# A graph layer on one core: output weights' halves added beside the ranking, and one block for storing the sums and the output

## The reference

```python
agg = segment_sum(res, col, num_segments=n) + segment_sum(res_i, row, num_segments=n)
h = jnp.concatenate([agg, agg], axis=1)
o = typed_linear(h, Wa, ba, node_type)      # Wa: (19, 512, 256), ba: (19, 256)
y = o + x
mu = y.mean(axis=-1, keepdims=True)
var = y.var(axis=-1, keepdims=True)
yn = (y - mu) / jnp.sqrt(var + LN_EPS)
return yn * gamma[node_type] + beta[node_type]
...
x = _layernorm(x + that, axis=-1)
```

## Time and profile before

| what | us |
|---|---|
| median of the three runs | 8410.45 |
| span of the profiled execution | 8400.1 |
| the time outside the span, median less span | 10.35 |
| ranking of edges | 456 to 2533 |
| storing the sums, output weights and bias | 8066.6 to 8127.7 |
| output: first gather to the first scatter | 8127.7 to 8166.4 |
| output: first scatter to the last but three | 8166.4 to 8365.6 |
| output: the rest | 8365.6 to 8400.1 |

### The profile page before, as it was taken

How to read it: one execution, slowest core, us unless ns; L and a number is a source line. 1 busy time by engine, 2 the same in 40 slices (tenths; PEclk the granted TensorE clock), 3 DMA queues, 4 the chain that set the end, 5 groups by cost and what they waited for, 6 DMA issues and landing times. The chain is left out here.

```text
span 8400.1 us, 132655 instructions
## 1 busy us (share of the span) xinstructions
PE 5523.3 (66%) x34292; PEld 3955.2 (47%) x34293; DVE 6052.2 (72%) x8967; ACT 4416.4 (53%) x12537; POOL 5874.8 (70%) x6077
## 2 busy tenths in 40 slices
PE   7766666666666667667766677613777772499944
PEld 6456666666663333333333333312555552388833
DVE  8377777777777878878777888744666663788865
ACT  0144444444445666666666666513666662388833
POOL 3657777777777777777777777756777771288835
PEclk5877777777778888888888888866999996699967
DMA  2553344333437988989988988977999999599963
GB/s 76 182 179 110 108 120 118 108 113 108 124 88 254 296 293 294 292 296 295 293 293 291 296 293 295 263 224 256 392 389 388 389 387 112 153 287 288 289 202 87
DMA packets 1586579, 1957.54 MB, mean 233 GB/s; under 512 B 429865, under 2 KB 1388307, under 8 KB 1586075
## 3 DMA queue, kind: packets, MB, share of 16 engines
q1 hardware_dynamic: 1083870, 1023.67, 40.0%
q0 software_dynamic: 255392, 674.52, 25.2%
q10 hardware_dynamic: 247072, 257.15, 9.0%
HBM read 1100.44 MB, written 883.21 MB: 236 GB/s over the span
## 5 line engine op out<-in xcount | busy, mean ns | idle before, releaser
L1141 PE MATMUL exch_pG<-far_tab,exch_ohT 128*128 x3328 | 1630.4, 643 | 625.7 <-ACT exch_kc L1056 621.4
L1002 POOL DMA_INDIRECT exch_row<-table,exch_of x1664 | 1598.6, 961 | 547.8 <-issue 520.3
L888 POOL DMA_INDIRECT recs<-place_rec,place_addr x1568 | 1570.8, 1002 | 540.4 <-issue 506.6
L1604 PE MATMUL sum_pS<-sum_row,sum_oh 128*128 128x260 f32 x6656 | 1620.2, 403 | 362.7 <-DVE edge_acc L1654 327.5
L1604 PEld LDWEIGHTS sum_pS<-sum_row,sum_oh 128*128 128x128 f32 x6656 | 1292.7, 199 | 689.9 <-DVE edge_acc L1654 407.6
L1141 PEld LDWEIGHTS exch_pG<-far_tab,exch_ohT 128*128 128x128 f32 x3328 | 747.3, 231 | 1458.2 <-issue 1411.8
L1216 POOL DMA_INDIRECT bys<-sum_pb x920 | 895.0, 973 | 296.6 <-issue 271.7
L1622 ACT ACTIVATE sum_off<-kept_ramp,sum_neg 128x128 f32<-128x128 f32 x3120 | 953.5, 387 | 92.4 <-POOL sum_neg L1559 92.4
L1055 ACT ACTIVATE exch_pb<-exch_pG 128x192 f32<-128x192 f32 x1664 | 551.1, 331 | 466.8 <-PE exch_pG L1141 399.5
L1216 POOL DMA_INDIRECT bys<-exch_pb x624 | 642.7, 1030 | 204.5 <-issue 158.1
L716 PE MATMUL place_pA<-place_t_lo 128*128 128x128 f16 x3136 | 313.1, 260 | 626.8 <-ACT place_t_lo L673 623.6
(11 more groups left out here) (319 smaller groups left out, 11940.1 us busy)
## 6 DMA issues: line engine op xcount, KB each, us to landing
bys<-place_none SPq DMA_DIRECT2D x52, 4224.0 KB
spill<-exch_row SPq DMA_DIRECT2D x208, 1024.0 KB
sum_row<-bys SPq DMA_DIRECT2D x208, 1024.0 KB, 5.3
sum_row<-spill ACTq DMA_DIRECT2D x206, 1024.0 KB
mid<-exch_pb SPq DMA_DIRECT2D x208, 660.0 KB
sum_pb<-mid SPq DMA_DIRECT2D x184, 660.0 KB
exch_row<-table,exch_of POOLq DMA_INDIRECT x1664
recs<-place_rec,place_addr POOLq DMA_INDIRECT x1568
```

The source lines that it names most:

```text
L888: nc.gpsimd.indirect_dma_start(recs, bass.IndirectOffsetOnAxis(addr[:, par, t:t + 1], 0), rec[:, par, t, :], None).then_inc(s_scat[par], 16)
L1002: nc.gpsimd.indirect_dma_start(row[q][:, t, TD:TD + S.TW], None, table, bass.IndirectOffsetOnAxis(of[q][:, t:t + 1], 0)).then_inc(s_row[q] ...
L1141: nc.tensor.matmul(pG[t % 3][:, 0:GW], ohT[ring(j, 2)][:, t, :], flat[:, bass.ds(tiles[t] * GW, GW)], start=True, stop=True).then_inc(s_ga ...
L1604: last = nc.tensor.matmul(pS[j % SETS * HG + t // 2][:, 0:AW], oh[h][:, t, :], row[j][:, t, :], start=(t % 2 == 0), stop=(t % 2 == 1))
```

## The change

Four things change together.

1. The halves of the output weights are added in `place_edges`. For 38 pieces (19 types, two parts of 128 rows) SyncE loads both halves to `wa`, VectorE adds them behind its work of a group, and SyncE stores the sum to `wsum` in memory, one group later. VectorE's loop over the groups becomes two loops, 38 groups with the addition and the others without.
2. `store_sums` is gone. Its stores, the bias and the load of the weights (now one half, from `wsum`) stand in `output`. Weights, gamma and beta are loaded when the sums have been stored, and gamma and beta go to the memory of the sums. GpSimd waits for the stores before it gathers, and TensorE waits for weights and bias before its first product.
3. z of batch b is made in turn b+2 of VectorE and no longer in turn b+1: a turn m now holds v(m-1), the start of batch m, and z(m-2). v and the second mean have two buffers each.
4. ScalarE makes two roots, one for each norm, straight from the sums of squares (scale and bias in the instruction), and the gather waits for the second mean of the batch that held the buffer, no longer for its z.

```diff
 place_edges, sync:
+            def halves(q):
+                t, h = divmod(q, S.OC)
+                if t:
+                    sp.wait_ge(s_ws[h], 16 * t)
+                for a in range(2):
+                    sp.dma_start(wa[h][:, a, :], Wa[t, a * S.OUT + h * P:a * S.OUT + (h + 1) * P, :]).then_inc(s_wl[h], 16)
+            def half_sum(q):
+                t, h = divmod(q, S.OC)
+                sp.wait_ge(s_wa[h], t + 1)
+                sp.dma_start(wsum[t, h * P:(h + 1) * P, :], wa[h][:, 0, :]).then_inc(s_ws[h], 16)
...
             for g in range(2, NG):
                 sp.wait_ge(s_rec, g - 1)
                 attributes(g)
+                if 2 <= g - 2 < S.T * S.OC:
+                    halves(g - 2)
+                elif g == 2:
+                    halves(0)
+                    halves(1)
+                if 0 <= g - 3 < S.T * S.OC:
+                    half_sum(g - 3)
...
 place_edges, vector:
-            in_turns(dve, NG, body)
+            def half_sums(h, i):
+                dve.wait_ge(s_wl[h], 32 * (i + 1))
+                nc.vector.tensor_tensor(wa[h][:, 0, :], wa[h][:, 0, :], wa[h][:, 1, :], ALU.add).then_inc(s_wa[h], 1)
+            with dve.Fori(0, S.T) as i:
+                for par in range(2):
+                    body(2 * i + par, par, i, True)
+                    half_sums(par, i)
...
 output, sync:
-            sp.dma_start(raw[:], bc(ba.rearrange("t n -> (t n)"), 0, 3)).then_inc(s_b, 16)
...
+            sp.dma_start(raw, bc(ba.rearrange("t n -> (t n)"), 0, 3)).then_inc(s_b, 16)
+            sp.wait_ge(s_o, STORED)
             for c in range(OC):
-                nc.scalar.dma_start(W[:, c], Wa[:, c * P:(c + 1) * P, :].rearrange("t p n -> p t n")).then_inc(s_w, 16)
-                nc.scalar.dma_start(W2[:, c], Wa[:, OUT + c * P:OUT + (c + 1) * P, :].rearrange("t p n -> p t n")).then_inc(s_w, 16)
+                sp.dma_start(W[:, c], wsum[:, c * P:(c + 1) * P, :].rearrange("t p n -> p t n")).then_inc(s_w, 16)
...
-            nc.vector.tensor_tensor(W, W, W2[:], ALU.add).then_inc(s_wr, 1)
...
 output, gpsimd:
-                    pool.wait_ge(s_z, n - RB + 1)
+                    pool.wait_ge(s_m1, n - RB + 1)
...
+            pool.wait_ge(s_o, STORED)
...
 output, tensor:
+                if n == 0:
+                    pe.wait_ge(s_b3, 1)
+                    pe.wait_ge(s_w, 16 * OC)
...
 output, vector:
+            for m in range(NBT + 2):
+                a, b = m - 1, m - 2
+                if 0 <= a < NBT:
+                    dve.wait_ge(s_r0, a + 1)
+                    last = nc.vector.reciprocal(inv[:, 0, :], root0[:])
+                if b >= 0:
+                    dve.wait_ge(s_r1, b + 1)
...
+                    last = nc.vector.reciprocal(inv[:, 1, :], root1[b % 2][:])
...
```

More of the change, by code:

```diff
@@ L612, in place_edges @@
         bq = s.sb("bq", [1, 3 * S.TD])
+        wa = [s.sb(f"wa{h}", [P, 2, S.IN]) for h in range(S.OC)]
+        s_wl, s_wa, s_ws = [[s.sem(f"{n}{h}") for h in range(S.OC)] for n in ("wl", "wa", "ws")]
+        assert S.OC == 2 and S.T < NG // 2 - 1
         s_none, s_clear, s_wb, s_blk, s_edge, s_tab, s_ang, s_two = [
@@ L667, in _ @@
             sp.wait_ge(s_ang, 16 * 4 * S.G)
+            for h in range(S.OC):
+                sp.wait_ge(s_ws[h], 16 * S.T)
         @block.scalar
@@ L1677, in _, with output @@
                 nc.vector.tensor_tensor(sums[:, :, a:a + w], sums[:, :, a:a + w], old[:, :, b:b + w], ALU.add)
-def store_sums(nc, k, S, total, joint, W, Wa, ba, b3, ones3):
-    OUT, NO, N, OC = S.OUT, S.NO, S.N, S.OC
+def output(nc, k, S, sums, W, wsum, joint, ba, gamma, beta, out):
+    T, OUT, IN, B, NBT, N, OC, NO = S.T, S.OUT, S.IN, S.B, S.NBT, S.N, S.OC, S.NO
     AW = S.VW + S.H
-    t = total[:].rearrange("p (o f) -> p o f", f=AW)
+    RB = 4
+    t = sums[:].rearrange("p (o f) -> p o f", f=AW)
@@ new lines, in output @@
+        ones3 = s.sb("ones3", [3, P], BF16)
+        row = [s.sb(f"row{n}", [P, B, OUT + IN]) for n in range(RB)]
+        aT = [s.sb(f"aT{n}", [P, B, OUT]) for n in range(2)]
+        work = s.sb("work", [P, 6, B, IN])
+        y, u, v, z = work[:, 0], work[:, 1], [work[:, 2 + n] for n in range(2)], [work[:, 4 + n] for n in range(2)]
+        raw = work[0:3].rearrange("p n b f -> p (n b f)")[:, 0:T * IN]
+        parts = s.sb("parts", [P, T * IN], BF16)
+        part = parts[0:3, :]
+        sq = parts[:].bitcast(F32)[:, 0:2 * B * IN].rearrange("p (a j n) -> p a j n", a=2, j=B)
@@ L1727, in output @@
[L1727 to L1750, removed]
-            s.sem(n) for n in ("par", "aT", "aTc", "p", "y", "z", "link", "m1", "m2", "q1", "q2", "var", "root", "turn")]
-        s_g = [s.sem(f"g{n}") for n in range(RB)]
-        s_sc = [s.sem(f"sc{h}") for h in range(2)]
-        block = ctx.enter_context(nc.Block())
-        @block.sync
-        def _(sp):
@@ L1840, in _ @@
                                                     accum_out=dev[:, 0, j:j + 1])
-                    last.then_inc(s_q1, 1)
-                act.wait_ge(s_var, m + 1)
-                nc.scalar.activation(root[:], var[:], ACT.Sqrt).then_inc(s_root, 1)
+                    last.then_inc(s_q0, 1)
+                    act.wait_ge(s_q0, m + 1)
+                    nc.scalar.activation(root0[:], dev[:, 0, :], ACT.Sqrt, scale=1.0 / IN, bias=eps[:]).then_inc(s_r0, 1)
         @block.vector
         def _(dve):
-            link, _ = chain(dve, s_link)
@@ L1848, in _ @@
[L1848 to L1854 removed]
+            link, _ = chain(dve, s_inv)
+            nc.vector.memset(eps[:], LN_EPS).then_inc(s_eps, 1)
+            nc.vector.memset(ones3[:], 1.0)
@@ new lines, in _ @@
+            nc.vector.tensor_scalar(less[:, 0:1], k.ident[0:3, 0:1], -1.0, None, ALU.add)
+            link(nc.vector.tensor_scalar(less[:, 1:2], k.ident[0:3, 2:3], -1.0, None, ALU.mult))
+            dve.wait_ge(s_b, 16)
+            for n in range(2):
+                link(nc.vector.tensor_copy(part, raw))
+                link(nc.vector.scalar_tensor_tensor(out=raw, in0=part, scalar=less[:, n:n + 1], in1=raw, op0=ALU.mult, op1=ALU.add))
+            nc.vector.tensor_copy(b3[:], raw).then_inc(s_b3, 1)
@@ L1863, in _ @@
                     dve.wait_ge(s_y, m + 1)
-                    nc.vector.tensor_scalar(mean[:, 0, :], total[:, 0, :], -1.0 / IN, None, ALU.mult).then_inc(s_m1, 1)
+                    nc.vector.tensor_scalar(mean0[:], total[:, 0, :], -1.0 / IN, None, ALU.mult).then_inc(s_m0, 1)
+                if b >= 0:
+                    if b >= 2:
+                        dve.wait_ge(s_sc[b % 2], 16 * B * (b // 2))
+                    if b < NBT - 1:
+                        dve.wait_ge(s_m1, b + 2)
+                    for j in range(B):
+                        last = nc.vector.tensor_scalar(z[b % 2][:, j, :], v[b % 2][:, j, :], mean1[b % 2][:, j:j + 1], inv[:, 1, j:j + 1],
+                                                       ALU.add, ALU.mult)
+                    last.then_inc(s_z, 1)
+                if m < NBT:
                     if m == 0:
```

123 lines of the change are left out of this document (57 added, 66 removed).

## The result

The changed kernel takes 8548.28 us (median of 4 runs, 8547.85 to 8549.27), the kernel before takes 8411.02 beside it (8409.65 to 8416.79): ratio 1.0164, 95% interval 1.0149 to 1.0178. The forecast was 8537 within 8512 to 8568, and slower.

What follows compares the result with a forecast made beforehand. GpSimd was taken to pace the ranking, and a ring through GpSimd, TensorE and VectorE the output loop. +148.0 - 20.3 - 2 + 1 = +126.7 on 8400.1, plus 10.35 outside the span, gave 8537 us, range 8512 to 8568.

Steps and rivals of the forecast that it cites:

- The ring: Output loop: scatter, gather, landing, transposes, matmuls, y, z, scatter bind every batch; 24.8 us a batch for 14.2, +148.0 us.
- Rival A: Output loop: the deeper pipeline hides the gather, GpSimd's issues pace it at 10.8 us a batch; about 8351 us, chance 6%.
- Rival B: Output loop: TensorE stays at the lower clock through each batch, 2 us a batch, 28 in all; 8565 us, chance 7%.
- The start: Output block up to scatter 0: sums stored first, beta landing last, scatter 0 at 8146.1 instead of 8166.41; -20.3 us.
- the bias split: Start of the output block: bias in three parts, ready at the latest at 8111.5, hidden by weights landing about 8113; no cost.
- The end: Scatter 14 to the end of the span: last three batches meet no gather, last z stands alone; -2 us (0 to -5).
- The ranking: Ranking of edges: 38 additions fit VectorE's 5 us of free time per group; +1 us.
- the 21 us between a load and the clearing store before it: Ranking, SyncE's queue: a load comes a group behind the last clearing store; spoke against loads being late.
- The bound of 16 us: Ranking: GpSimd pays only if a busier VectorE slows its issues, 0 to 38 x 0.42 = 16 us.
- groups that grow: Ranking: 21.2 us per group was to stay the same; longer groups would show the forecast wrong.
- Rival C: Ranking: each of 38 sums holds its group a microsecond beside its 0.42, +40 to +55; about 8580 us, chance 4%.
- The 10.35 us outside the span: Whole kernel: median 8410.45 less span 8400.1, taken as time outside the span and added at the end.

Runs made afterwards that it cites:

- z ahead of y: Changed kernel with z of batch b made at the head of VectorE's turn b+2, ahead of v and y: 8399.44 us, ratio 0.9992 to the kernel before.
- TensorE's order: Changed kernel with TensorE multiplying batch n before it transposes batch n+1: 8400.48 us, ratio 0.9984 to the kernel before.
- five and six buffers: Changed kernel with 5 or 6 row buffers in place of 4, so gathers are issued one or two pairs earlier: 8379.8 us and 8354.62 us.
- the control: Kernel before, run and profiled again with no edit: 8406.59 us, ratio 1.0001, profile span 8410.8 us.
- the sums later: Changed kernel with the 38 sums of halves ten groups later in the ranking: 8510.84 us; with six row buffers as well: 8319.20 us.

## Where the prediction was right and where not

**The ring, right to a microsecond.** +147.4 us, forecast +148.0; each step is within 0.6 us of its row. Two edits undo it from different sides (z ahead of y, TensorE's order), and buffers scale it as a ring must: some 25 us for one batch, then for two, then GpSimd's own pace. Rival A would have needed z not to wait for the gather in front of it; with six buffers that holds, and its price, 10.8 us a batch, came out as 10.6. "DMA: Bandwidth & Descriptors" of the Trainium skill, "Rules for kernel authors", to issue early and wait late, holds here for the kernels with five and six buffers: more batches in flight pay only when the gather is issued earlier too. Rival B is false as well: tiles took 1.56 and then 1.13 us in the batch above (8332.10, 8333.80), behind an idle time of 16.7 us. In five of the loop's batches the second tile was slow too (1.36 to 2.08 us), the third and fourth in none.

**The start, right in sum, wrong in its parts.** -20.1 us, forecast -20.3. These are rows of the timeline, GpSimd and VectorE:

```profile
8114.39 1.08 POOL L1782 DMA_INDIRECT out_row<-joint,kept_rows  x1 [58.20 <-DMA joint<-acc_acc]
8115.00 2.95 DVE L1871 CAST out_parts<-out_work 3x4864 bf16<-3x4864 f32 x1 [23.93 <-DMA out_work<-in_L_gnn_ba]
8115.77 3.00 POOL L1782 DMA_INDIRECT out_row<-joint,kept_rows  x1 [0.30 <-issue]
...
8119.08 7.01 POOL L1782 DMA_INDIRECT out_row<-joint,kept_rows  x1 [0.30 <-issue]
8123.29 2.68 DVE L1871 CAST out_parts<-out_work 3x4864 bf16<-3x4864 f32 x1
...
8126.40 7.72 POOL L1782 DMA_INDIRECT out_row<-joint,kept_rows  x1 [0.31 <-issue]
8131.31 2.68 DVE L1873 CAST out_b<-out_work 3x4864 bf16<-3x4864 f32 x1
...
8149.66 0.42 DVE L1900 SCALAR_TENSOR_TENSOR out_work<-out_row,out_pP 128x256 f32<-128x256 f32 x1 [15.68 <-PE out_pP L1828]
...
8154.03 1.43 DVE L1918 TENSOR_TENSOR out_row<-out_row,acc_acc 128x256 f32<-128x256 f32 x4 [0.85 <-DMA acc_acc<-in_L_gnn_beta]
```

The sums had landed 23.7 us behind the block's begin (forecast 21.9), beta at +63.3 (60.7), and from there to scatter 0 it took 16.3 us (18.8). Beta came last, as said, but by 0.85 us only. y(0) began at 8149.66, because three of the first four gathers took 3.00, 7.01 and 7.72 us to issue beside the bias split on VectorE, and the rows of batch 1 landed late (TensorE's transposes of it start at 8143.84, after a wait of 2.2 us for them). The forecast had taken the bias split, hidden behind the weights, as free. It is free only by those 0.85 us.

**The end.** -3.9, within its bounds of 0 to -5.

**The ranking, mis-sized: +17 for +1.** The step that failed is "the 21 us between a load and the clearing store before it", from a steady stretch (1500 to 1540). The first sum is not in a steady stretch. Its load stands behind the small transfers of the ranking's start, and its own block waits in order on VectorE for it. The bound of 16 us was taken for another cause, a slower GpSimd, which did not come: the 95 later groups cost 2.3 us together. So one of the forecast's signs of being wrong, groups that grow, showed in the first three groups and in no others. Rival C had the right place, a load late behind the queue, but priced it for all 38 sums; only the first was held.

**The exchange, +10.6 for 0.** No part of the change was found to cause it, and the control shows stretches without an edit moving as far. Against the control's profile (8410.8) the changed kernel's is 136.7 us longer, and that is the difference of the medians, 137.3.

**The 10.35 us outside the span, wrong.** It was no overhead. A timed execution is 1.8 us longer than its span (8549.27 and 8547.5 in the profiled one); the other 8.6 were the difference between one short execution of the kernel before, which is none of the timed ones, and their median. Adding 10.35 made up for half of the 20.7 us by which the span's forecast was short (8526.8 against 8547.5), so that the total was off by 11 us instead of some 20. That closeness is luck. The range would have held without the 8.6 us too (8503 to 8559).

## What to carry to other kernels

When a result moves one batch later in the order of an engine, follow the in-order queues back to the issue that it now waits for: what counts is not how many batches are in flight but how many pairs of issues lie between a gather and the scatter that hangs on it. A buffer more, which lets the gather be issued a pair earlier, was worth 50 us to the kernel before, and 164 to the changed one. Once one engine's order is mended, look for the next one that closes the same ring, here ScalarE's. And work hidden beside a loop must be looked at in the loop's first turns, where its loads stand behind everything that the queue does at the start.

## What the hardware showed beside it

**Long issues on two queues.** A gather's issue on GpSimd took 0.95 us in the loop, and 3.00, 7.01 and 7.72 us at the block's start (rows above). Busy DMA engines alone don't make it long. In the kernel before, 16 gathers took 0.94 to 1.08 us each in this stretch, with the DMA engines full (columns of the earlier trace rows):

```profile
8127.70:8150.00 22.30, 9.25 (x34) 6.72 (x35) 0.77 (x4) 2.39 (x4) 15.27 (x16) 0.56 1.02 375
```

VectorE was busy for 0.77 us there. In the changed kernel it splits the bias, and the issues of 3.00, 7.01 and 7.72 us end 0.8, 0.1 and 0.1 us behind the end of a cast. That VectorE's instructions hold them up is argued from these times; no run moved the split away. A small load's issue on SyncE took 14.27 us behind the clearing stores, and no run shows what ends it.

**Two patterns of GpSimd beside VectorE in an untouched loop.** In the second aggregation GpSimd copies 128x8 elements, on which ScalarE waits, and later multiplies 128x448, while VectorE works beside it. The first two rows are of the changed kernel, the two below of the one with the sums later (ns minimum, median, maximum; first and last start):

```profile
L1596 POOL COPY sum_neg<-edge_less x208: 179/1320/1609, 7287.3 to 8052.9; 128x8 f32 x102, 128x8 f32<-128x8 f32 x2
L1604 POOL TENSOR_TENSOR sum_row<-sum_row,agg_al x208: 925/936/2017, 7289.8 to 8055.3; 128x448 f32<-128x448 f32 x104
```

```profile
L1600 POOL COPY sum_neg<-edge_less x208: 182/186/1444, 7272.2 to 8021.2; 128x8 f32 x102, 128x8 f32<-128x8 f32 x2
L1608 POOL TENSOR_TENSOR sum_row<-sum_row,agg_al x208: 927/2112/2330, 7274.7 to 8022.5; 128x448 f32<-128x448 f32 x104
```

In one pattern the copy takes 1.32 us and the multiplication 0.94; in the other 0.19 and 2.11. Since ScalarE waits for the copy (95.2 us in all in the changed kernel, 75.8 with the sums later), the second is shorter, 749 against 766 us for the loop. That is the missing 17 us. Both kernels with the sums later had the second pattern, the eleven other profiles the first (median of the copy 1.29 to 1.45 us). That the time is held up by VectorE is only argued: "SBUF — State Buffer" of the Trainium skill, section "SBUF: two separate sides", says that VectorE and GpSimd share a pair of ports and that the loser waits for the whole instruction, which fits that an excess of 1.2 us moves from one instruction to the other, but no run here took VectorE away. What sets the pattern stays open too.
